# Routed feed-forward stage of a decoder: the gates are laid on 128 rows by transfers, in place of selector products

## The chip, the cores and the metric

The kernel runs on one core of a Trainium2 chip. Its engines are TensorE (PE; its weight loads are shown apart as PEld), VectorE (DVE), ScalarE (ACT), GpSimd (POOL) and the queue engine SyncE (SP), which here only issues transfers (DMA). On-chip memory (SBUF) has 128 rows, called partitions; products land in a second memory (PSUM) of eight banks. The metric is the time of the whole program in device microseconds. A trace is one profiled execution; its span is the time from its first to its last instruction.

## The reference, cut to what matters

The input is x of 16 sequences, 128 tokens, 256 features. Six residual blocks follow, each with a layer norm. The change lies in the third, a feed-forward block with two shared experts of 128 hidden values each and sixteen routed experts of 64:

```python
gs = jnp.einsum('td,ndm->tnm', flat, wg_s)
us = jnp.einsum('td,ndm->tnm', flat, wu_s)
out = jnp.einsum('tnm,nmd->td', jax.nn.silu(gs) * us, wd_s)
logits = (flat @ router_w).astype(jnp.float32)
probs = jax.nn.softmax(logits, axis=-1)
weights, indices = jax.lax.top_k(probs, TOP_K)      # TOP_K = 2 of 16
weights = weights / (weights.sum(axis=-1, keepdims=True) + 1e-09)
comb = jnp.sum(jax.nn.one_hot(indices, N_ROUTED, dtype=x.dtype) * weights[..., None], axis=1)
g = jnp.einsum('td,edm->tem', flat, wg_r)
u = jnp.einsum('td,edm->tem', flat, wu_r)
h = jax.nn.silu(g) * u
h = h * comb[:, :, None]
out = out + jnp.einsum('tem,emd->td', h, wd_r)
```

`comb` is the gate of each token and expert. All sixteen experts are computed for all tokens, and the gate makes most of them zero.

## The kernel before, in words

Each of the six blocks is a stage; the order inside a stage is written out by hand, and semaphores tie the engines together. The routed stage (names `F3` and `f3...`) works in four groups of four sequences, 512 tokens each. Features lie on the partitions, tokens along the row: `f3XT` is x transposed. The hidden values, 256 of the shared and 1024 of the routed experts, are cut into ten chunks of 128 rows: chunks 0 and 1 are shared, chunks 2 to 9 hold two routed experts each, 64 rows per expert. Every product is made of three products of high and low parts (`split3`, lines 85 to 87), so an up step is 12 products of 512 columns and a down step 12 of 256.

The list that `ffn_order` returns is walked by PE, ACT and DVE alike. For chunk c its steps are "u" (PE: up products; ACT: silu into `f3gs`), before the change "s" for c from 2 on (PE: `spread`), "t" (DVE: `product`), "d" of chunk c-2 (PE: down products) and "h" of chunk c-1 (ACT writes the high part `f3hT_h`, DVE the low part `f3hT_l`). So on DVE the low part of chunk c-1 stands behind the product of chunk c, and on PE the down products of c-1 need that low part.

The gates: PE computes the router's logits at a group's start ("l"), ACT and DVE the softmax and the top two ("e", "r"). After chunk 1, PE transposes them (line 1325) to 16 rows of 512 tokens, and DVE copies them from PSUM to `combT` in two parts, high (line 1457) and low (line 1458), on rows 0 to 15 and 32 to 47. `spread` (line 1299) multiplies `combT` by a selector `f3sel` of zeros and ones that puts the gates of experts 2(c-2) and 2(c-2)+1 on 64 rows each. The result lies in a PSUM bank, and `product` makes `f3tt` = silu times up (line 1446) and then `f3h` = `f3tt` times that bank (line 1450). GpSimd and VectorE build the selector in the stage before; `combT` is set to zero once.

SP's program before the stage loads `w_a4` (the next attention's weights) in four pieces; DVE splits them in group 0 after chunks 4 to 7. Piece k may be loaded when piece k-2 is split. Then, once for each of groups 1 to 3, SP copies the next group's x into `f3Xs` (line 1228), which PE transposes after chunk 9 of the group ahead. In the last group, PE also transposes the next stage's x and computes its first keys and queries among the chunks; SP then lays those on partitions (line 1683), 16 partitions per transfer.

Of the kernel before, what the change touches and what calls it, by code (L numbers as in the profile page):

```python
# [89 lines left out]
def program(nc, x_in, ctxT_in, itokT_in, w_a1, w_e1i, w_e1o, w_ffn, w_a4, w_a5, w_e6i, w_e6o,  # L90
# [912 lines left out]
    def mix_vector(v, c, parts, beside=None, between=None):  # L1003
# [138 lines left out]
    F3.gs = m.place("f3gs", [P, 2, GT], F32)  # L1142
    F3.tt = m.place("f3tt", [P, 2, GT], F32)
    F3.h32 = m.place("f3h32", [P, 2, GT], F32)
    F3.combT = m.place("f3combT", [P, GT], F32R)
    F3.lg = m.place("f3lg", [P, GB, R_N], F32)
    F3.pr = m.place("f3pr", [P, GB, R_N + 6], F32)
    F3.mr = m.place("f3mr", [P, GB, R_N + 6], F32)
# [16 lines left out]

    def ffn_order(first, last):

        order = [("l", 0), ("e", 0)]
        if not first:
            order.append(("a", 0))
        order.append(("r", 0))
        for c in range(FC + 1):
            if c < FC:
                x = [("x", k) for k in range(DC)] if last and c == FC - 4 else []
                k = [("nk", k) for k in range(DC)] if last and c == FC - 2 else []
                order += x[:1] + k[:1] + ([("nk evac", 0)] if k else []) + [("u", c)] + x[1:] + k[1:]
                order += ([("s", c)] if c >= SC else []) + ([("nq", 0)] if last and c == FC - 1 else []) + [("t", c)]  # L1180
# [28 lines left out]

        return g * FG + (DC + k + 3)  # L1210

    FL, FT, FX = 0, 1, 2 + FC - SC

    def ffn_last(g):
        return type(g) is int and g == NG - 1

    def ffn_x(g, ch):

        return (FX - 4 if ffn_last(g) else FX) + ch

    def ffn_spread(g, c):
        return c + (DC if ffn_last(g) and c >= FC - 4 else 0)

    def ffn_sync(sp):
        s = F3.s
        with sp.Fori(1, NG) as g:
            sp.wait_ge(s["xt_hi"], g * DC + C1)
            sp.dma_start(F3.Xs[:, :, :], X[:, bass.ds(g * GB, GB), :]).then_inc(s["xs_loaded"], 16)

    def ffn_selector_pool(pool):  # L1230
        s = F3.s

        nc.gpsimd.memset(F3.sel32[:, :, :], 0.0).then_inc(s["sel_pool"], 1)
        pool.wait_ge(s["sel_pool"], 1)
        sel = F3.sel32[:, :, :].rearrange("e c (a m) -> e c a m", a=2)
        for n, row in enumerate((0, LO_ROWS)):
            nc.gpsimd.affine_select(out=sel, in_=sel, compare_op=ALU.not_equal, fill=1.0, base=-row,
                                    pattern=[[-2, FC - SC], [-1, 2], [0, R_MID]], channel_multiplier=1).then_inc(s["sel_pool"], 1)
            if n == 0:
                pool.wait_ge(s["sel_pool"], 2)  # L1240
# [34 lines left out]
    def ffn_tensor(pe, first_keys, first_queries):  # L1275
# [16 lines left out]
        def spread(g, c):

            bank = g_fill(g, ffn_spread(g, c))
            if ffn_last(g) and c >= FC - 2:
                pe.wait_ge(N.s["g_evac"], n_filled(0, NK + c - (FC - 2)))
            if c == SC:
                pe.wait_ge(s["g_evac"], ffn_evac(g, FT))
            nc.tensor.matmul(bank, F3.sel[:, c - SC, :], F3.combT[:, :], start=True, stop=True).then_inc(s["g_full"], 1)

        def down(g, c):
            pe.wait_ge(s["h_ready"], g * FC + c + 1 + C1)
            if c == 0:
# [24 lines left out]
        def steps(g, order):  # L1328
            for kind, c in order:
                if kind == "x":  # L1330
                    transposed_x(g, c)
                elif kind == "l":
                    logits(g)
                elif kind == "u":
                    up(g, c)
                elif kind == "c":
                    gates_transposed(g)
                elif kind == "s":
                    spread(g, c)
                elif kind == "d":  # L1340
                    down(g, c)
                elif kind == "nk":
                    first_keys(c)
                elif kind == "nq":
                    first_queries(c)

        pe.wait_ge(s["sel_ready"], 1)
        ffn_groups(pe, steps)

    def ffn_scalar(act):  # L1350
# [9 lines left out]
        def steps(g, order):  # L1360
            for kind, c in order:
                if kind == "x":
                    transposed_x(g, c)
                elif kind == "e":
                    act.wait_ge(s["g_evac"], ffn_evac(g, FL))
                    nc.scalar.activation(F3.pr[:, :, 0:R_N], F3.lg[:, :, :], ACT.Exp).then_inc(s["soft_exp"], 1)
                elif kind == "u":
                    act.wait_ge(s["gu_full"], g * FC + c + 1)
                    nc.scalar.activation(F3.gs[:, c % 2, :], ps[:, c % 2, :], ACT.Silu).then_inc(s["sg_ready"], 1)
                elif kind == "h":  # L1370
                    if c < SC:
                        act.wait_ge(s["t_done"], g * FC + c + 3)
                    else:
                        act.wait_ge(s["g_evac"], ffn_evac(g, ffn_spread(g, c)))
                    nc.scalar.activation(F3.hT[0][:, c % 3, :], F3.h32[:, c % 2, :], ACT.Identity).then_inc(s["hi_ready"], 1)
                elif kind in ("nk evac", "nq evac"):
                    n_hi_qk(act, 0, kind[1], c)
# [1 line left out]
        for ch in range(DC):  # L1379
            transposed_x(-1, ch)  # L1380
        ffn_groups(act, steps)

    def ffn_selector(v):
        v.wait_ge(F3.s["sel_pool"], 3)
        nc.vector.tensor_copy(F3.sel[:, :, :], F3.sel32[:, :, :]).then_inc(F3.s["sel_ready"], 1)

    def ffn_transposed_x(v, g, ch):
        s = F3.s
# [13 lines left out]
    def ffn_vector_begin(v, ch):  # L1402
        s = F3.s
        if ch == 0:
            nc.vector.memset(F3.combT[:, :].bitcast(F32), 0.0).then_inc(s["sel_ready"], 1)
            nc.vector.memset(F3.pr[:, :, R_N:], -1.0).then_inc(s["sel_ready"], 1)
            v.wait_ge(s["sel_ready"], 3)
        ffn_transposed_x(v, -1, ch)

    def ffn_vector(v, link, of_mixture, following):  # L1410
# [31 lines left out]
        def product(g, c):  # L1442
# [2 lines left out]
            dst = F3.h32 if c < SC else F3.tt  # L1445
            nc.vector.tensor_tensor(dst[:, c % 2, :], F3.gs[:, c % 2, :], ps[:, 2 + c % 2, :], ALU.mult).then_inc(s["t_done"], 1)
            if c >= SC:
                v.wait_ge(s["g_full"], ffn_full(g, ffn_spread(g, c)))
                v.wait_ge(s["t_done"], g * FC + c + 3)
                nc.vector.tensor_tensor(F3.h32[:, c % 2, :], F3.tt[:, c % 2, :], ps[:, 4 + c % 2, :], ALU.mult).then_inc(s["g_evac"], 1)  # L1450
                v.wait_ge(s["g_evac"], ffn_evac(g, ffn_spread(g, c)))

        def gates_transposed(g):
            v.wait_ge(s["g_full"], ffn_full(g, FT))
            src = ps[0:R_N, 4 + FT % 2, :]
            hi, lo = F3.combT[0:R_N, :], F3.combT[LO_ROWS:LO_ROWS + R_N, :]
# [317 lines left out]
    def n_projections(pe):  # L1774
# [370 lines left out]
    with block as block:  # L2145
        @block.sync
        def _(sp):
# [57 lines left out]
        def _(pool):  # L2205
# [62 lines left out]
        def _(v):  # L2268
# [129 lines left out]
```

## Time and profile before

| | |
|---|---|
| median of 3 runs | 1560.12 us (1559.51 to 1562.1) |
| the profiled execution | 1562.81 us, its span 1560.8 us |
| share of the span: PE, PEld, DVE, ACT, POOL | 97%, 84%, 63%, 47%, 13% |
| mean granted clock of TensorE | 0.989 of full speed |
| routed stage | about 679 to 884 us of the span |

Busy PE time is the union of its products, whose ends are modelled: what one product costs in a dense row of products is the distance from its start to the next one's start, not its duration.

### The profile page before, as it was taken

Reading aid. Unit: us, or ns where it says so; the run is one execution under the profiler, and the core shown is the slowest. Engines: PE = TensorE matmul, PEld = TensorE weight load, DVE = VectorE, ACT = ScalarE, POOL = GpSimd, SP = SyncE. Lnnn points to the kernel's source line nnn. Section 1 sums busy time; section 2 is a strip of 40 time slices with the busy share of each in tenths; the row PEclk is TensorE's granted clock in tenths of the full one; section 3 lists DMA queues with packets and bytes.
Section 4 is the critical chain, followed back from the end, with each engine's and each line's share of the span. In section 5 each row is a group of like instructions: output and inputs, shape, how many; then the busy total and the mean of one; then the engine's idle time right before and its main releaser. Section 6 shows DMA issues by size and latency. Waiting matters only on the chain.

```text
span 1560.8 us, 28560 instructions
## 1 busy us (share of the span) xinstructions
PE 1514.9 (97%) x10996; PEld 1316.0 (84%) x11018; DVE 988.6 (63%) x2131; ACT 729.8 (47%) x1874; POOL 203.7 (13%) x215
## 2 busy tenths in 40 slices
PE   7999999899999999999999999999998999999997
PEld 6898988789999999978888867777766988999886
DVE  6777777864554555576666567788886464444547
ACT  4766666622222222223323367788884444444443
POOL 1322322310000000030000034212221300000001
PEclk9999999999999999999999999999999999999999
DMA  6000100011010101100000585677750000000001
GB/s 217 1 15 1 42 2 1 28 40 41 26 36 19 52 27 39 34 1 34 1 13 1 74 139 67 86 101 134 105 79 28 1 28 28 28 27 27 27 0 54
DMA packets 43080, 66.50 MB, mean 43 GB/s; under 512 B 4576, under 2 KB 33504, under 8 KB 42848
## 3 DMA queue, kind: packets, MB, share of 16 engines
q1 hardware_dynamic: 42976, 65.09, 20.0%
q8 instruction: 68, 1.11, 0.3%
q14 instruction: 36, 0.29, 0.1%
HBM read 36.24 MB, written 2.10 MB: 25 GB/s over the span
## 4 chain that ended last, share of the span: by engine, by line
PE 90%; DVE 6%; ACT 2%; issue 1%; DMA 1%; POOL 0%; SPq 0%; DVEq 0%; POOLq 0%; ACTq 0%
PE ps L85 23%; PE ps L86 22%; PE ps L87 22%; PE ps L1859 3%; PE ps L1873 3%; PE ps L1849 2%; PE ps L392 2%; PE ps L404 2%; PE ps L417 2%; PE ps L1904 2%; PE ps L1887 1%; ACT wPr L472 1%; PE ps L1846 1%; PE ps L1895 1%; PE ps L1823 0%
## 5 line engine op out<-in xcount | busy, mean ns | idle before, releaser
L858 ACT ACTIVATE m2hT_h<-ps 128x512 fp32r<-128x512 f32 x128 | 76.7, 599 | 281.4 <-PE ps L87 281.4
L982 DVE TENSOR_TENSOR m6hT_l<-m6h,m6hT_h 128x512 fp32r<-128x512 f32 x128 | 88.5, 691 | 169.5 <-ACT m6hT_h L856 169.5
L984 DVE SCALAR_TENSOR_TENSOR m2hT_l<-ps,m2hT_h 128x512 fp32r<-128x512 f32 x128 | 88.4, 691 | 163.4 <-ACT m2hT_h L858 163.4
L855 ACT ACTIVATE m6h<-ps,m6b 128x512 f32<-128x512 f32 x128 | 88.4, 691 | 202.5 <-PE ps L87 196.2
L1985 ACT ACTIVATE nPr<-ps,negm 128x128 f32<-128x128 f32 x512 | 147.2, 383 | 26.2 <-DVE negm L2088 25.3
L87 PE MATMUL ps<-w_h,m6hT_l 128*128 128x256 f32 x512 | 144.4, 282 | 0.0
L85 PE MATMUL ps<-w_h,m6hT_h 128*128 128x256 f32 x512 | 143.0, 279 | 0.7 <-DVE m6hT_l L982 0.7
L86 PE MATMUL ps<-w_l,m6hT_h 128*128 128x256 f32 x512 | 143.6, 280 | 0.0
L87 PE MATMUL ps<-m2w_h,m2hT_l 128*128 128x256 f32 x448 | 126.8, 283 | 0.0
L86 PE MATMUL ps<-m2w_l,m2hT_h 128*128 128x256 f32 x448 | 126.7, 283 | 0.0
L85 PE MATMUL ps<-m2w_h,m2hT_h 128*128 128x256 f32 x448 | 126.3, 282 | 0.0
L2088 DVE TENSOR_REDUCE negm<-ps 128x4 f32<-128x512 f32 x128 | 88.2, 689 | 48.1 <-PE ps L1849 47.6
L85 PE MATMUL ps<-m6XT_h,w_h 128*128 128x512 f32 x256 | 103.3, 404 | 2.1 <-DVE m6hT_l L982 2.1
L87 PE MATMUL ps<-m6XT_h,w_l 128*128 128x512 f32 x256 | 102.1, 399 | 0.0
L85 PEld LDWEIGHTS ps<-w_h,m6hT_h 128*128 128x128 f32 x512 | 96.7, 189 | 5.9 <-DVE m6hT_l L982 0.9
L86 PE MATMUL ps<-m6XT_l,w_h 128*128 128x512 f32 x256 | 101.3, 396 | 0.0
L86 PEld LDWEIGHTS ps<-w_l,m6hT_h 128*128 128x128 f32 x512 | 96.2, 188 | 5.7
L892 POOL TENSOR_TENSOR rstd<-veps,mhalf 128x4 f32<-128x4 f32 (+1 forms) x9 | 9.7, 1074 | 684.2 <-DVE veps L1041 679.3
L472 ACT ACTIVATE wPr<-ps,negm 128x128 f32<-128x128 f32 x256 | 90.3, 372 | 14.7 <-DVE negm L553 14.7
L87 PEld LDWEIGHTS ps<-w_h,m6hT_l 128*128 128x128 f32 x512 | 96.2, 188 | 0.0
L85 PEld LDWEIGHTS ps<-m2w_h,m2hT_h 128*128 128x128 f32 x448 | 85.5, 191 | 4.8
L317 POOL TENSOR_TENSOR wPr<-wPr,wrec 128x512 f32<-128x512 f32 x64 | 65.9, 1050 | 180.8 <-DVE wrec L558 180.8
(322 smaller groups left out, 4323.6 us busy)
## 6 DMA issues: line engine op xcount, KB each, us to landing
nKm<-nKc_h SPq DMA_DIRECT2D x64, 128.0 KB, 4.5
nQs<-nQc_h SPq DMA_DIRECT2D x64, 128.0 KB, 5.7
raw<-in_w_e1i SPq DMA_DIRECT2D x9, 512.0 KB, 3.2
raw<-in_w_e1o SPq DMA_DIRECT2D x9, 512.0 KB, 3.3
raw<-in_w_e6i SPq DMA_DIRECT2D x9, 512.0 KB, 3.3
raw<-in_w_e6o SPq DMA_DIRECT2D x9, 512.0 KB, 3.3
nKm<-nKc_l SPq DMA_DIRECT2D x32, 128.0 KB, 5.2
nQs<-nQc_l SPq DMA_DIRECT2D x32, 128.0 KB, 6.0
```

The costliest lines, as they stand in the source:

```text
L85: nc.tensor.matmul(out, wh, xh, start=start, stop=False, **kw)
L86: nc.tensor.matmul(out, wh, xl, start=False, stop=False, **kw)
L87: return nc.tensor.matmul(out, wl, xh, start=False, stop=stop, **kw)
L317: nc.gpsimd.tensor_tensor(own, own, scale.unsqueeze(2).broadcast_to([P, QH, S]), ALU.mult).then_inc(s["p_ready"], 1)
L472: last = nc.scalar.activation(W.Pr[:, p % 3, half, j, :], ps[:, WSB[half], j * S:(j + 1) * S], ACT.Exp, bias=negm[:, n % 4, j:j + 1], accu ...
L855: nc.scalar.activation(c.h32[:, u % 2, :], ps[:, u % 2, :], ACT.Gelu, bias=bias)
L858: nc.scalar.activation(c.hT[0][:, ch, :], ps[:, u % 2, :], ACT.Relu).then_inc(c.s["hi_ready"], 1)
L982: last = nc.vector.tensor_tensor(c.hT[1][:, ch, :], c.h32[:, u % 2, :], c.hT[0][:, ch, :].bitcast(F32), ALU.subtract)
L984: last = nc.vector.scalar_tensor_tensor(c.hT[1][:, ch, :], ps[:, u % 2, :], 0.0, c.hT[0][:, ch, :].bitcast(F32), ALU.max, ALU.subtract)
L1859: last = nc.tensor.transpose(ps[:, TB[n % 2], i * S:(i + 1) * S], N.Pr[:, n % 4, i, :], ident[:, :])
L1985: last = nc.scalar.activation(N.Pr[:, i % 4, j, :], ps[:, SB[i % 2], j * S:(j + 1) * S], ACT.Exp, bias=negm[:, i % 4, j:j + 1])
L2088: nc.vector.reduce_max(negm[:, i % 4, :], ps[:, SB[i % 2], :].rearrange("p (h k) -> p h k", h=QH), AX.X, negate=True).then_inc(s["s_max"], 1)
```

## The change

PE no longer multiplies by a selector. DVE copies the transposed gates to rows 0 to 15 of `combT` in one piece. For each routed chunk, SP issues one transfer that reads two rows of `combT` 64 times each and writes 128 rows of 2 KB. There are six targets: four for chunks 2 to 5 and two that chunks 6 to 9 share, so the transfers of chunks 8 and 9 wait until the product of chunk c-2 has read its target. `product` waits for the transfer's semaphore and reads SBUF in place of PSUM. The selector and its building are gone, and with them the waits of the first keys and queries for the spread banks.

```diff
-    F3.combT = m.place("f3combT", [P, GT], F32R)
+    F3.combT = m.place("f3combT", [P, GT], F32)
...
-    F3.sel32 = m2.place("f3sel32", [P, FC - SC, P], F32)
-    F3.sel = r1b.place("f3sel", [P, FC - SC, P], F32R)
+    NGT = 6
...
+    gates4 = Region(nc, n_x0_at, 8 * KB).place("f3gates4", [P, 4, GT], F32)
+    gates2 = r1b.place("f3gates2", [P, 2, GT], F32)
+    F3.gate = [gates4[:, i, :] for i in range(4)] + [gates2[:, i, :] for i in range(2)]
+    F3.laid = [sem(f"f3_laid{i}") for i in range(NGT)]
...
-                order += ([("s", c)] if c >= SC else []) + ([("nq", 0)] if last and c == FC - 1 else []) + [("t", c)]
+                order += ([("nq", 0)] if last and c == FC - 1 else []) + [("t", c)]
...
+    def ffn_gated(g, c):
+
+        return F3.s["gated"], g * (FC - SC) + (c - SC + 1)
+
+    def ffn_place(c):
+
+        i = c - SC
+        return (i, 0, 1) if i < 4 else (4 + i % 2, (i - 4) // 2, 2)
+
+    def ffn_lay_gates(sp, g, chunks):
+        s = F3.s
+        if chunks[0] == SC:
+            sp.wait_ge(s["g_evac"], ffn_evac(g, FT))
+        for c in chunks:
+            i, load, _ = ffn_place(c)
+            if load:
+                sp.wait_ge(*ffn_gated(g, c - 2))
+            rows2 = F3.combT[2 * (c - SC):2 * (c - SC) + 2, :]
+            sp.dma_start(F3.gate[i], rows2.unsqueeze(1).broadcast_to([2, R_MID, GT])).then_inc(F3.laid[i], 16)
 
     def ffn_sync(sp):
         s = F3.s
-        with sp.Fori(1, NG) as g:
+        sp.wait_ge(s["xt_hi"], DC + C1)
+        sp.dma_start(F3.Xs[:, :, :], X[:, GB:2 * GB, :]).then_inc(s["xs_loaded"], 16)
+        with sp.Fori(2, NG) as g:
             sp.wait_ge(s["xt_hi"], g * DC + C1)
             sp.dma_start(F3.Xs[:, :, :], X[:, bass.ds(g * GB, GB), :]).then_inc(s["xs_loaded"], 16)
...
+            ffn_lay_gates(sp, g - 1, range(SC, FC))
+        ffn_lay_gates(sp, NG - 1, range(SC, FC))
...
-            nc.tensor.matmul(bank, F3.sel[:, c - SC, :], F3.combT[:, :], start=True, stop=True).then_inc(s["g_full"], 1)
...
-            nc.vector.memset(F3.combT[:, :].bitcast(F32), 0.0).then_inc(s["sel_ready"], 1)
...
             if c >= SC:
-                v.wait_ge(s["g_full"], ffn_full(g, ffn_spread(g, c)))
+                i, load, loads = ffn_place(c)
+                v.wait_ge(F3.laid[i], g * (16 * loads) + 16 * (load + 1))
                 v.wait_ge(s["t_done"], g * FC + c + 3)
-                nc.vector.tensor_tensor(F3.h32[:, c % 2, :], F3.tt[:, c % 2, :], ps[:, 4 + c % 2, :], ALU.mult).then_inc(s["g_evac"], 1)
-                v.wait_ge(s["g_evac"], ffn_evac(g, ffn_spread(g, c)))
+                nc.vector.tensor_tensor(F3.h32[:, c % 2, :], F3.tt[:, c % 2, :], F3.gate[i], ALU.mult).then_inc(s["gated"], 1)
+                v.wait_ge(*ffn_gated(g, c))
...
-            link(nc.vector.tensor_copy(hi, src))
-            nc.vector.tensor_tensor(lo, src, hi.bitcast(F32), ALU.subtract).then_inc(s["g_evac"], 1)
+            nc.vector.tensor_copy(F3.combT[0:R_N, :], src).then_inc(s["g_evac"], 1)
...
                 load_unit(sp, U_A4, k, w_a4[:, at:at + n], n)
+                if k == 1:
+                    ffn_lay_gates(sp, 0, range(SC, FC - 2))
+            ffn_lay_gates(sp, 0, range(FC - 2, FC))
             sp.wait_ge(stage_done, 2)
             ffn_sync(sp)
```

On SP, from the next attention's weights (`raw<-in_w_a`) to the end of the stage's x copies, the program before reads:

```order
43 L679 DMA raw_50<-in_w_a 128x768
44 L679 DMA raw_51<-in_w_a 128x768
45 L679 DMA raw_50<-in_w_a 128x256
46 L679 DMA raw_51<-in_w_a 128x256
47 L1226 UNCONDITIONAL_BRANCH
48 L1226 ISA
49 L1228 ISA
50 L1228 DMA f3Xs<-X 128x1024
```

and the changed one (`f3gates_160` are the four targets of chunks 2 to 5, `f3gates_161` the two of chunks 6 to 9; what a row waits for is in brackets):

```order
43 L679 DMA raw_50<-in_w_a 128x768 [waits prep_done]
44 L679 DMA raw_51<-in_w_a 128x768 [waits prep_done]
45 L1243 DMA f3gates_160<-f3combT 128x1x512 [waits f3_g_evac]
46 L1243 DMA f3gates_160<-f3combT 128x1x512 x3
47 L1243 DMA f3gates_161<-f3combT 128x1x512 x2
48 L679 DMA raw_50<-in_w_a 128x256 [waits prep_done]
49 L679 DMA raw_51<-in_w_a 128x256 [waits prep_done]
50 L1243 DMA f3gates_161<-f3combT 128x1x512 [waits f3_gated] x2
51 L1248 DMA f3Xs<-X 128x1024 [waits f3_xt_hi,stage_done]
```

Six gate transfers of group 0 now stand ahead of the last two weight pieces, and two more ahead of the first copy of x, which stood right behind the weights before.

On DVE, in group 0 from the copy of the transposed gates to the product of chunk 3, before:

```order
639 L1457 CAST f3combT<-ps 16x512
640 L1458 TENSOR_TENSOR f3combT<-ps,f3combT 16x512
641 L1524 TENSOR_TENSOR f3hT_l<-f3h_148,f3hT_h 128x512
642 L1446 TENSOR_TENSOR f3tt<-f3gs,ps 128x512
643 L1450 TENSOR_TENSOR f3h_148<-f3tt,ps 128x512
644 L1524 TENSOR_TENSOR f3hT_l<-f3h_148,f3hT_h 128x512
```

and changed:

```order
637 L1453 COPY f3combT<-ps 16x512
638 L1519 TENSOR_TENSOR f3hT_l<-f3h_148,f3hT_h 128x512
639 L1442 TENSOR_TENSOR f3tt<-f3gs,ps 128x512
640 L1447 TENSOR_TENSOR f3h_148<-f3tt,f3gates_160 128x512
641 L1519 TENSOR_TENSOR f3hT_l<-f3h_148,f3hT_h 128x512
```

One of the two copies is gone, and the product with the gates (line 1450 before, 1447 now) reads the laid gates; the low part of the chunk before stands behind it as it did.

On PE, at the end of the up products of chunk 2 in group 0, before:

```order
2722 L86 MATMUL ps<-f3XT_l,wF_h 128x512
2723 L87 MATMUL ps<-f3XT_h,wF_l 128x512
2724 L1299 MATMUL ps<-f3combT,f3sel 128x512
2725 L85 MATMUL ps<-wF_h,f3hT_h 128x256
2726 L86 MATMUL ps<-wF_l,f3hT_h 128x256
```

and changed:

```order
2719 L86 MATMUL ps<-f3XT_l,wF_h 128x512
2720 L87 MATMUL ps<-f3XT_h,wF_l 128x512
2721 L85 MATMUL ps<-f3XT_h,wF_h 128x512
2722 L86 MATMUL ps<-f3XT_l,wF_h 128x512
2723 L87 MATMUL ps<-f3XT_h,wF_l 128x512
2724 L85 MATMUL ps<-wF_h,f3hT_h 128x256
2725 L86 MATMUL ps<-wF_l,f3hT_h 128x256
```

The down products of chunk 0 now follow the up products directly; the same holds at the other 31 places.

## Rows read from the trace of the kernel before

**Rows 1.** The page: busy time of PE, and the chain that ended last.

```profile
PE 1514.9 (97%) x10996; PEld 1316.0 (84%) x11018; DVE 988.6 (63%) x2131; ACT 729.8 (47%) x1874; POOL 203.7 (13%) x215
PE 90%; DVE 6%; ACT 2%; issue 1%; DMA 1%; POOL 0%; SPq 0%; DVEq 0%; POOLq 0%; ACTq 0%
```

**Rows 2.** Stretch 690 to 884 us: busy time by engine, granted clock, DMA share, GB/s.

```profile
690.00:884.00 194.00, 190.72 (x1084) 164.40 (x1085) 119.45 (x270) 60.81 (x100) 12.83 (x6) 0.99 0.05 16
```

**Rows 3.** Waits of PE in that stretch: us in total, times, longest.

```profile
PE ps L85 <- DVE f3h L1446: 2.7, 3, 1.9
PE ps L85 <- DVE f3hT_l L1524: 0.8, 3, 0.3
```

**Rows 4.** PE in order of time around two selector products (start, duration), and their group.

```profile
753.38 0.40 PE L1299 MATMUL ps<-f3combT,f3sel 128*128 128x512 f32 x1
753.62 0.29 PE L85 MATMUL ps<-wF_h,f3hT_h 128*128 128x256 f32 x1
...
757.82 0.40 PE L1299 MATMUL ps<-f3combT,f3sel 128*128 128x512 f32 x1
...
L1299 PE MATMUL ps<-f3combT,f3sel 128*128 128x512 f32 x32 | 12.7, 398 | 0.0
```

**Rows 5.** DVE in order of time: copy of the gates, product of chunk 9, groups 0 to 3.

```profile
692.57 0.68 DVE L1457 CAST f3combT<-ps 16x512 fp32r<-16x512 f32 x1
...
727.99 0.69 DVE L1450 TENSOR_TENSOR f3h<-f3tt,ps 128x512 f32<-128x512 f32 x1
...
742.07 0.67 DVE L1457 CAST f3combT<-ps 16x512 fp32r<-16x512 f32 x1
...
777.21 0.69 DVE L1450 TENSOR_TENSOR f3h<-f3tt,ps 128x512 f32<-128x512 f32 x1
...
791.00 0.67 DVE L1457 CAST f3combT<-ps 16x512 fp32r<-16x512 f32 x1
...
826.17 0.69 DVE L1450 TENSOR_TENSOR f3h<-f3tt,ps 128x512 f32<-128x512 f32 x1
...
839.82 0.67 DVE L1457 CAST f3combT<-ps 16x512 fp32r<-16x512 f32 x1
...
878.39 0.69 DVE L1450 TENSOR_TENSOR f3h<-f3tt,ps 128x512 f32<-128x512 f32 x1
```

**Rows 6.** End of group 2 in order of time, DVE and PE.

```profile
826.89 0.69 DVE L1524 TENSOR_TENSOR f3hT_l<-f3h,f3hT_h 128x512 fp32r<-128x512 f32 x1
...
829.59 0.39 PE L85 MATMUL ps<-wF_h,f3hT_h 128*128 128x256 f32 x1 [0.26 <-DVE f3hT_l L1524]
```

**Rows 7.** Transfers, 779 to 782 us: packets, MB, share of 16 engines; time to landing.

```profile
q1 hardware_dynamic: 144, 0.52, 43.1%
f3Xs<-X SPq DMA_DIRECT2D x1, 512.0 KB, 2.9
```

**Rows 8.** Transfers, 1011 to 1016 us: GB/s in 40 slices, then as in rows 7.

```profile
GB/s 131 172 139 131 106 123 98 107 90 164 164 123 115 115 123 90 98 123 180 139 123 115 106 115 98 98 148 156 156 131 98 106 107 90 131 164 148 123 115 115
DMA packets 684, 0.62 MB, mean 124 GB/s; under 512 B 77, under 2 KB 684, under 8 KB 684
q1 hardware_dynamic: 684, 0.62, 117.5%
```

**Rows 9.** Busy time and granted clock (seventh number) around a wait of PE.

```profile
687.90:691.30 3.40, 1.23 (x7) 0.88 (x8) 3.33 (x13) 0.63 (x1) 1.01 (x1) 1.00 0.01 2
691.30:694.70 3.40, 3.40 (x10) 2.63 (x9) 3.17 (x7) 0.00 (x0) 2.17 (x1) 0.53 0.00 0
694.70:698.10 3.40, 3.40 (x21) 3.02 (x20) 2.05 (x3) 1.12 (x2) 3.40 (x1) 0.97 0.00 0
```

**Rows 10.** PE in order of time in the slow stretch.

```profile
692.20 0.63 PE L87 MATMUL ps<-f3XT_h,wF_l 128*128 128x512 f32 x1
692.63 0.63 PE L85 MATMUL ps<-f3XT_h,wF_h 128*128 128x512 f32 x1
```

**Rows 11.** The selector's copy on DVE: duration in ns, start in us.

```profile
L1385 DVE CAST f3sel<-f3sel x1: 684/684/684, 404.7 to 404.7; 128x1024 fp32r<-128x1024 f32 x1
```

More of the change, by code:

```diff
@@ L1154, in program @@
     F3.r = m.place("f3r", [P, GB, D], F32)
-    m2 = Region(nc, M2.end, r2.end - M2.end)
-    F3.sel32 = m2.place("f3sel32", [P, FC - SC, P], F32)
-    F3.sel = r1b.place("f3sel", [P, FC - SC, P], F32R)
+    NGT = 6
+    n_x0_at = r2.start + 45120
+    assert m.at <= n_x0_at
+    gates4 = Region(nc, n_x0_at, 8 * KB).place("f3gates4", [P, 4, GT], F32)
+    gates2 = r1b.place("f3gates2", [P, 2, GT], F32)
+    F3.gate = [gates4[:, i, :] for i in range(4)] + [gates2[:, i, :] for i in range(2)]
+    F3.laid = [sem(f"f3_laid{i}") for i in range(NGT)]
     F3.s = signals("f3", "xs_loaded xt_hi g_full g_evac soft_exp comb_ready gu_full sg_ready t_done hi_ready h_ready "
-                         "d_full r_done ln_var rstd_ready x_done sel_pool sel_ready")
+                         "d_full r_done ln_var rstd_ready x_done gated pad_ready")
     assert m.at <= n_at
-    FG = 2 + FC - SC + DC
-    LO_ROWS = 32
-    F_LINKS = 19 + 2 * GB
+    FG = 2 + DC
+    F_LINKS = 18 + 2 * GB
     def ffn_order(first, last):
@@ L1210, in ffn_evac @@
         return g * FG + (DC + k + 3)
-    FL, FT, FX = 0, 1, 2 + FC - SC
+    FL, FT, FX = 0, 1, 2
     def ffn_last(g):
@@ L1217, in ffn_x @@
     def ffn_x(g, ch):
-        return (FX - 4 if ffn_last(g) else FX) + ch
-    def ffn_spread(g, c):
-        return c + (DC if ffn_last(g) and c >= FC - 4 else 0)
+        return FX + ch
+    def ffn_gated(g, c):
[13 more added lines that the diff above has]
+            sp.dma_start(F3.gate[i], rows2.unsqueeze(1).broadcast_to([2, R_MID, GT])).then_inc(F3.laid[i], 16)
     def ffn_sync(sp):
         s = F3.s
-        with sp.Fori(1, NG) as g:
+        sp.wait_ge(s["xt_hi"], DC + C1)
+        sp.dma_start(F3.Xs[:, :, :], X[:, GB:2 * GB, :]).then_inc(s["xs_loaded"], 16)
+        with sp.Fori(2, NG) as g:
             sp.wait_ge(s["xt_hi"], g * DC + C1)
             sp.dma_start(F3.Xs[:, :, :], X[:, bass.ds(g * GB, GB), :]).then_inc(s["xs_loaded"], 16)
[L1230 to L1240, printed above, removed]
+            ffn_lay_gates(sp, g - 1, range(SC, FC))
+        ffn_lay_gates(sp, NG - 1, range(SC, FC))
     def ffn_pool(pool):
@@ L1290, in up @@
             last.then_inc(s["gu_full"], 1)
[L1292 to L1298, printed above, removed]
-            nc.tensor.matmul(bank, F3.sel[:, c - SC, :], F3.combT[:, :], start=True, stop=True).then_inc(s["g_full"], 1)
         def down(g, c):
@@ L1337, in steps @@
                     gates_transposed(g)
-                elif kind == "s":
-                    spread(g, c)
                 elif kind == "d":
@@ L1345, in steps @@
                     first_queries(c)
-        pe.wait_ge(s["sel_ready"], 1)
         ffn_groups(pe, steps)
@@ L1373, in steps @@
                     else:
-                        act.wait_ge(s["g_evac"], ffn_evac(g, ffn_spread(g, c)))
+                        act.wait_ge(*ffn_gated(g, c))
                     nc.scalar.activation(F3.hT[0][:, c % 3, :], F3.h32[:, c % 2, :], ACT.Identity).then_inc(s["hi_ready"], 1)
@@ L1381, in ffn_scalar @@
         ffn_groups(act, steps)
-    def ffn_selector(v):
-        v.wait_ge(F3.s["sel_pool"], 3)
-        nc.vector.tensor_copy(F3.sel[:, :, :], F3.sel32[:, :, :]).then_inc(F3.s["sel_ready"], 1)
     def ffn_transposed_x(v, g, ch):
@@ L1404, in ffn_vector_begin @@
         if ch == 0:
-            nc.vector.memset(F3.combT[:, :].bitcast(F32), 0.0).then_inc(s["sel_ready"], 1)
-            nc.vector.memset(F3.pr[:, :, R_N:], -1.0).then_inc(s["sel_ready"], 1)
-            v.wait_ge(s["sel_ready"], 3)
+            nc.vector.memset(F3.pr[:, :, R_N:], -1.0).then_inc(s["pad_ready"], 1)
+            v.wait_ge(s["pad_ready"], 1)
         ffn_transposed_x(v, -1, ch)
@@ L1455, in gates_transposed @@
             src = ps[0:R_N, 4 + FT % 2, :]
-            hi, lo = F3.combT[0:R_N, :], F3.combT[LO_ROWS:LO_ROWS + R_N, :]
-            link(nc.vector.tensor_copy(hi, src))
-            nc.vector.tensor_tensor(lo, src, hi.bitcast(F32), ALU.subtract).then_inc(s["g_evac"], 1)
+            nc.vector.tensor_copy(F3.combT[0:R_N, :], src).then_inc(s["g_evac"], 1)
         def sums_of(g):
@@ L1801, in first_keys @@
                 pe.wait_ge(prep_done, U_A5)
-            pe.wait_ge(F3.s["g_evac"], ffn_evac(NG - 1, ffn_spread(NG - 1, FC - 4 + ch)))
             project(0, "k", A4.wk, ch, *of_x(0))
         def first_queries(ch):
-            pe.wait_ge(F3.s["g_evac"], ffn_evac(NG - 1, ffn_spread(NG - 1, FC - 2 + ch)))
             project(0, "q", A4.wq, ch, *of_x(0))
@@ L2225, in _ @@
             pool.wait_ge(stage_done, 1)
-            ffn_selector_pool(pool)
             mix_pool(pool, M2)
@@ L2319, in _ @@
             v.sem_inc(stage_done, 1)
-            of_mixture = mix_vector(v, M2, m2, lambda: (ffn_selector(v), ffn_vector_start(v)), lambda ch: ffn_vector_begin(v, ch))
+            of_mixture = mix_vector(v, M2, m2, lambda: ffn_vector_start(v), lambda ch: ffn_vector_begin(v, ch))
             def start_n():
```

## Prediction

> **What bounds the kernel now.** I read the page first: PE is busy for 97% of the span and makes up 90% of the chain that ended last [rows 1]. Then the stretch of the routed stage: from 690 to 884 us PE is busy for 190.7 of 194 us, DVE for 119, ACT for 61, and the transfer engines for 5% [rows 2]. The waits of PE there come to 2.7 us for the first products of each group and 0.8 us for the last low parts of `f3hT` [rows 3]. So PE bounds the stage, DVE has room, and the transfers hardly exist. An instruction taken off PE is time gained, unless something takes PE's place.
>
> **What is removed.** From a selector product to the product behind it PE takes 753.62 - 753.38 = 0.24 us (its duration of 0.40 overlaps with its neighbours), and there are 32 of them [rows 4]: 32 x 0.235 = 7.5 us. One chunk now takes 757.82 - 753.38 = 4.44 us and would take 4.20. DVE's second copy of the gates (as long as the first, 0.67 us, four times), the clearing of `combT` and the selector's copy [rows 11] go too, and GpSimd's building of it. I cost these at nothing: PE does not wait for the copies (its next step needs the product of chunk 0, ahead of them), and the selector's copy, 0.68 us at 404 us, lies in a stage where PE bounds too. Should they be on the path, they are at most 4 x 0.67 + 0.7 for the selector and no more than 0.7 for the clearing (as long a row as other steps of 0.69), 4.1 us more of gain.
>
> **What is added.** Per group eight transfers of 128 x 2 KB = 256 KB each, issued by SP when DVE has copied the gates. Call the time from one landing to the next T, and the fixed part of a transfer F. F comes from the copy of x into `f3Xs`: 512 KB in 2.9 us from issue to landing, with 0.431 x 16 x 3 us = 20.7 us of engine time, so 25.3 GB/s for each engine and 1.3 us for its share [rows 7]. F = 2.9 - 1.3 = 1.6 us, and 0.1 for SP's wait: 1.7. The gates of chunk 9 land 1.7 + 8T after the copy of the gates ends.
>
> What waits: DVE's product with the gates of chunk c. Behind it on DVE stand the low part of chunk c-1 and the product of c+1; PE's down products of c-1 need that low part. On SP the transfers of chunks 8 and 9 wait for the products of chunks 6 and 7, and what stands behind them waits too. In the middle of a group there is slack, at the end there is none: PE begins the last down step 829.59 - 826.17 = 3.4 us after the product of chunk 9 and even waits 0.26 us for it [rows 5, 6]. So a group is longer by what the last product is later.
>
> From the end of the gates' (first) copy to the product of chunk 9 there are now 727.99 - 693.25 = 34.7, 777.21 - 742.74 = 34.5, 826.17 - 791.67 = 34.5 and 878.39 - 840.49 = 37.9 us [rows 5], in sum 141.6 us (the last group holds work of the next stage). Without selector products they would be shorter by 7.5 in all. With transfers that are slower than PE the sum is 4 x (1.7 + 8T). The break-even lies near T = 4.2 us, or 63 GB/s for one transfer.
>
> **How large is T?** No row shows a transfer that reads two rows 64 times. Lower bound: all 16 engines at their 25.3 GB/s, 256 KB / 405 GB/s = 0.65 us. Upper bound: transfers that write 16 neighbouring partitions. They run at a mean of 124 GB/s with the engines more than fully taken (117.5%) [rows 8], 7.8 GB/s for each partition; two partitions at that rate give 16.9 us. Which is nearest? [...] The two rows that a gate transfer reads are neighbours (2(c-2) and the next), thus most likely behind one door, however many engines fetch: T = 256 KB / 25.3 GB/s, about 10.3 us. I take that. [...]
>
> [...]
>
> **The sum.** 4 x (1.7 + 82.4) - 141.6 = 194.8 us. Group 0 adds two things. The two weight pieces now stand between the gates of chunks 7 and 8 and share the transfer engines: 2 x 128 KB at 16 engines, 0.7 us. And the first `f3Xs` copy, which had stood ahead, follows the gates of chunk 9; PE's transposes wait for it, and with them ACT's and DVE's copies that stand ahead of the last high and low part: 1.6 us. That is 197.1. **PE's clock**: PE stands for most of each group, some 6 us between a chunk's 4.2 us of work. The trace shows what follows: after a stretch in which PE was busy for 1.23 of 3.40 us the granted clock is 0.53, so mostly the 1.2 GHz level, and full again after it [rows 9]; products of 512 columns then come every 0.43 us, not 0.23 [rows 10]. Inside a group half clock is hidden, since 4.2 x 0.43 / 0.23 = 7.9 us of work still fit into 10.3. At each end the two last down steps (12 x 0.12 = 1.4 us each) and the start of what follows run at it: about 1.8 us, four times, 7 us. In all +204 us. The profiled execution took 1562.8 (span 1560.8 and 2.0 around it), 2.7 above the median of 1560.1; the change applies to either, so 1560.1 + 204 = **1764 us**, +13%.
>
> **Rivals.** (1) *Two engines, two doors.* The source's outermost count is 2 (rows), the target's 128. If the work is split by the outermost count, two engines fetch one row each at 25.3 GB/s: 128 KB each, T = 5.2 us. If the two rows do not share a door, the sum is 4 x (1.7 + 41.6) - 141.6 + 2.3 = +33.9 us, 1594 us, and PE's idle time of 1 us a chunk leaves the clock up. For it: rows 8 speak of writes alone. [...]
>
> (2) *Transfers hidden: faster.* If all 16 engines take part and neighbours do not share, T = 0.65 us plus SP's issue. The gates of chunk 2 land 1.7 + 0.65 = 2.4 us after the copy; the product with them is due 34.5 - 7 x 4.44 = 3.4 us after it [rows 4, 5], and PE gains its 7.5 us: 1552.6 us. It decides for T below 4.2. For it: the transfer engines are idle for 95% of the stage [rows 2], and one such engine is fast. Against: it needs 63 GB/s out of two neighbouring rows, 2.5 times what one engine shows.
>
> (3) *Concentration as bad as in rows 8 per partition.* T = 16.9: 4 x (1.7 + 135) - 141.6 + 2.3 = +408 us, with the clock about 1975 us.
>
> (4) *No measurable change*: a T of 4.1 to 4.3 us. Nothing in the rows points there.
>
> **Chances.** My forecast (T of 9.5 to 11) 0.66; two doors 0.20; between 5.6 and 9.5 us 0.04; worse than 11 us 0.05; hidden 0.04; no change 0.01. What a measurement of this kernel tells from no change is about 0.2%. So slower 0.95, same 0.01, faster 0.04. The forecast's own range goes from T = 9.6 with little loss by the clock (4 x 78.5 - 141.6 + 2.3 = +175, 1735) to T = 10.8 and twice that loss (about 1795). Since it holds but two thirds, the range takes in the case of two doors, 1588 to 1604: 1588 to 1795, a wide gap with little in the middle.
>
> **What will show it.** PE: no line of selector products; the busy share of the stage at some 45% and long waits of its down products for the low part `f3hT_l` (right), or none (rival 2). DVE: idle ahead of the product that reads `f3gates`, released by the transfer, some 6 us for each chunk (1 us in rival 1), growing from the first chunk on. The chain that ended last: some 330 us of transfers `f3gates<-f3combT` in it. Transfers: few engines busy (2 of 16, a share of 0.12, if the work is split by the outermost count) and about 25 GB/s through the stage, 50 in rival 1. Landings: the sixth of a burst some 6 x 10.3 us after issue. The clock at 0.5 for parts of the stage. Stages before 690 us should stay as they are. I am wrong if reads of neighbours are not limited as writes are, or if a fetch of the same row 64 times is served in some faster way.

## The result, and the profile after

The changed kernel takes a median of 1763.28 us (1762.01 to 1767.86, 4 runs), beside 1561.11 us (1559.51 to 1564.08, 4 runs) for the kernel before: a ratio of 1.1298, 95% interval 1.127 to 1.1326. The forecast was 1764. The profiled execution took 1762.22 us with a span of 1760.4, 199.6 more than the span before.

The page of the changed kernel: busy time, PE and the granted clock in 40 slices, the chain that ended last, and two groups with the idle time ahead of them behind the second bar.

```profile
PE 1560.9 (89%) x10986; PEld 1352.6 (77%) x10986; DVE 983.9 (56%) x2125; ACT 731.3 (42%) x1874; POOL 200.4 (11%) x212
...
PE   7999998999999997656576667899999899999997
...
PEclk9999999999999999777787878999999999999999
...
PE 72%; DMA 14%; SPq 6%; DVE 5%; ACT 2%; issue 1%; POOL 0%; DVEq 0%; POOLq 0%; ACTq 0%
PE ps L85 18%; PE ps L86 18%; PE ps L87 18%; DMA f3gates<-f3combT 11%; SPq L1243 5%; PE ps L1852 3%; PE ps L1866 2%; DMA raw<-in_w_a 2%; PE ps L392 2%; PE ps L1842 2%; PE ps L1897 2%; PE ps L417 2%; PE ps L404 2%; DMA f3Xs<-X 1%; PE ps L1880 1%
...
L85 PE MATMUL ps<-wF_h,f3hT_h 128*128 128x256 f32 x160 | 64.7, 404 | 145.6 <-DVE f3hT_l L1519 145.6
...
L1447 DVE TENSOR_TENSOR f3h<-f3tt,f3gates 128x512 f32<-128x512 f32 x32 | 22.1, 692 | 236.6 <-DMA f3gates<-f3combT 236.5
```

PE was the chain by 90% [rows 1] and is 72% now. The gates' transfers (11%) and SP's issue of them (line 1243, 5%), 282 us together, stand in it. PE waits 145.6 us for the low parts `f3hT_l`, and DVE, one step earlier, 236.5 us for the gates. Beside [rows 3] and [rows 5], where PE waited 0.8 us for those low parts and DVE's product came from PSUM, that is the new wait.

The waits of the stretch 690 to 1090 us: engine, line, waited for, us in total, times, longest.

```profile
DVE f3h L1447 <- DMA f3gates<-f3combT: 236.5, 31, 10.7
...
PE ps L85 <- DVE f3hT_l L1519: 145.6, 30, 11.9
```

DVE in order of time, as in [rows 5], with the first products of group 1.

```profile
690.91 0.68 DVE L1453 COPY f3combT<-ps 16x512 f32<-16x512 f32 x1
...
777.73 0.69 DVE L1447 TENSOR_TENSOR f3h<-f3tt,f3gates 128x512 f32<-128x512 f32 x1 [7.67 <-DMA f3gates<-f3combT]
...
793.22 0.67 DVE L1453 COPY f3combT<-ps 16x512 f32<-16x512 f32 x1
...
806.23 0.69 DVE L1447 TENSOR_TENSOR f3h<-f3tt,f3gates 128x512 f32<-128x512 f32 x1 [8.96 <-DMA f3gates<-f3combT]
...
817.09 0.69 DVE L1447 TENSOR_TENSOR f3h<-f3tt,f3gates 128x512 f32<-128x512 f32 x1 [8.65 <-DMA f3gates<-f3combT]
...
879.01 0.69 DVE L1447 TENSOR_TENSOR f3h<-f3tt,f3gates 128x512 f32<-128x512 f32 x1 [7.79 <-DMA f3gates<-f3combT]
...
894.23 0.67 DVE L1453 COPY f3combT<-ps 16x512 f32<-16x512 f32 x1
...
979.14 0.69 DVE L1447 TENSOR_TENSOR f3h<-f3tt,f3gates 128x512 f32<-128x512 f32 x1 [7.35 <-DMA f3gates<-f3combT]
...
993.82 0.67 DVE L1453 COPY f3combT<-ps 16x512 f32<-16x512 f32 x1
...
1079.88 0.69 DVE L1447 TENSOR_TENSOR f3h<-f3tt,f3gates 128x512 f32<-128x512 f32 x1 [7.79 <-DMA f3gates<-f3combT]
```

In group 1 the first product comes 806.23 - 793.89 = 12.3 us after the copy's end, the eighth 72.8 us later: a transfer lands every 72.8 / 7 = 10.4 us. 31 of the 32 products wait for their own transfer, so DVE and PE merely follow. (The one that doesn't is that of chunk 7 in group 0, where DVE splits weights meanwhile.)

The transfers from 800 to 840 us, as in [rows 7].

```profile
DMA packets 502, 1.03 MB, mean 26 GB/s; under 512 B 8, under 2 KB 8, under 8 KB 500
...
q1 hardware_dynamic: 500, 1.01, 11.9%
```

26 GB/s with 11.9% of the engine time used: two of sixteen engines, hardly ever idle, would show 12.5%.

The stage in windows, columns as in [rows 2] (the seventh number is the granted clock), with three pieces of 3.4 us around one wait.

```profile
806.90:810.30 3.40, 2.59 (x12) 2.60 (x13) 1.40 (x3) 0.63 (x1) 0.00 (x0) 0.50 0.14 30
810.30:813.70 3.40, 3.40 (x11) 2.68 (x11) 0.00 (x0) 0.00 (x0) 0.00 (x0) 0.54 0.12 25
813.70:817.10 3.40, 1.06 (x5) 0.54 (x3) 0.01 (x1) 0.60 (x1) 0.00 (x0) 0.97 0.13 28
690.00:1088.00 398.00, 243.60 (x1061) 205.44 (x1059) 114.64 (x265) 62.86 (x99) 11.82 (x5) 0.78 0.13 30
```

After a wait, 145.6 / 30 = 4.9 us on average, PE begins a chunk's work mostly at half clock (0.50, then 0.54) and is granted the full clock (0.97) only when that work is nearly over. Over the whole stage the clock is 0.78, against 0.99 [rows 2].

### The profile page after: what moved, and what is told of

It is laid out like the page before. It is cut to its first block, busy times and chain, and to the rows that moved or that the text cites. A ratio compares the mean times of both kernels' runs of the same rounds, so it can differ in the third digit from the quotient of the medians.

```text
span 1760.4 us, 28524 instructions
## 1 busy us (share of the span) xinstructions
PE 1560.9 (89%) x10986; PEld 1352.6 (77%) x10986; DVE 983.9 (56%) x2125; ACT 731.3 (42%) x1874; POOL 200.4 (11%) x212
## 4 chain that ended last, share of the span: by engine, by line
PE 72%; DMA 14%; SPq 6%; DVE 5%; ACT 2%; issue 1%; POOL 0%; DVEq 0%; POOLq 0%; ACTq 0%
PE ps L85 18%; PE ps L86 18%; PE ps L87 18%; DMA f3gates<-f3combT 11%; SPq L1243 5%; PE ps L1852 3%; PE ps L1866 2%; DMA raw<-in_w_a 2%; PE ps L392 2%; PE ps L1842 2%; PE ps L1897 2%; PE ps L417 2%; PE ps L404 2%; DMA f3Xs<-X 1%; PE ps L1880 1%
## 5 line engine op out<-in xcount | busy, mean ns | idle before, releaser
L85 PE MATMUL ps<-wF_h,f3hT_h 128*128 128x256 f32 x160 | 64.7, 404 | 145.6 <-DVE f3hT_l L1519 145.6
L85 PEld LDWEIGHTS ps<-wF_h,f3hT_h 128*128 128x128 f32 x160 | 44.9, 280 | 158.7 <-DVE f3hT_l L1519 158.5
L1447 DVE TENSOR_TENSOR f3h<-f3tt,f3gates 128x512 f32<-128x512 f32 x32 | 22.1, 692 | 236.6 <-DMA f3gates<-f3combT 236.5
L1370 ACT ACTIVATE f3gs<-ps 128x512 f32<-128x512 f32 x40 | 23.9, 597 | 189.2 <-PE ps L87 189.2
```

Source lines behind the costliest of these rows:

```text
L85: nc.tensor.matmul(out, wh, xh, start=start, stop=False, **kw)
```

## The experiments

Each edit below is a difference to the changed kernel. Two questions are open after the result: is it the rows' place or the count of engines that holds a transfer at 25 GB/s, and did PE's 7.5 us come off at all? A time without a range is that of a single run; the time beside a result is that of the kernel before on the same chip.

**`e1_rows8`: the two rows of a chunk 8 apart.** DVE's last router product writes the gates in another order, so that the transposed rows of a chunk's two experts are i and i+8. One transfer still carries both.

```diff
...
-            rows2 = F3.combT[2 * (c - SC):2 * (c - SC) + 2, :]
+            rows2 = F3.combT[c - SC:c - SC + 9:8, :]
...
+            apart = F3.comb[:, :, :].rearrange("p b (j i) -> p b i j", j=2)
+            own = F3.own[:, :, :].rearrange("p b (i j) -> p b i j", j=2)
...
```

> The gates are transposed in another order, so that the two experts of a chunk stand on rows 8 apart (i and i+8) and not side by side; the transfers are otherwise the changed kernel's. [...] Theory 'row' (a row that is fetched again and again gives only 12.8 GB/s, or each of the two engines is slow by itself): T stays at 10.4 us and the total at 1763 us.

Measured: 1600.55 us (1600.27 to 1601.77, 4 runs) beside 1560.55, a ratio of 1.0264 (1.0234 to 1.0294). That is 6.6 us above the 1594 that rival 1 works out with T = 5.2 us, and far below the 1763 of theory 'row'. Its transfers from 700 to 720 us, and DVE in group 2:

```profile
DMA packets 575, 1.09 MB, mean 55 GB/s; under 512 B 11, under 2 KB 86, under 8 KB 574
...
q1 hardware_dynamic: 574, 1.08, 14.3%
```

```profile
811.04 0.67 DVE L1457 COPY f3combT<-ps 16x512 f32<-16x512 f32 x1
...
829.19 0.69 DVE L1451 TENSOR_TENSOR f3h<-f3tt,f3gates 128x512 f32<-128x512 f32 x1 [1.11 <-DMA f3gates<-f3combT]
834.46 0.69 DVE L1451 TENSOR_TENSOR f3h<-f3tt,f3gates 128x512 f32<-128x512 f32 x1 [1.68 <-DMA f3gates<-f3combT]
...
855.09 0.69 DVE L1451 TENSOR_TENSOR f3h<-f3tt,f3gates 128x512 f32<-128x512 f32 x1 [2.94 <-DMA f3gates<-f3combT]
```

Twice the rate (the slices of that view read 49 to 53 GB/s but for a few with other transfers), still with about the share of two engines; a landing every 5.2 us ((855.09 - 818.65) / 7, from the first product of the group to the eighth). Four fifths of the loss are gone by the place of a row alone.

**`e2_rows33` and `e2b_rows65`: how far apart.** DVE copies the rows twice, to rows 0 to 15 and to 32 to 47 (or 64 to 79), and the transfer takes its second row from the second copy.

```diff
-            rows2 = F3.combT[2 * (c - SC):2 * (c - SC) + 2, :]
+            r = 2 * (c - SC)
+            rows2 = F3.combT[r:r + 34:33, :]
...
+            link(nc.vector.tensor_copy(F3.combT[0:R_N, :], src))
+            nc.vector.tensor_copy(F3.combT[32:32 + R_N, :], src).then_inc(s["g_evac"], 1)
```

> VectorE writes the gates' rows twice, to rows 0 to 15 and to rows 32 to 47 (0.7 us more per group), and each transfer takes its first row from the first and its second from the second copy, 33 rows apart. [...]

> As the run with rows 33 apart, but the second copy of the gates stands on rows 64 to 79 and the two rows of a transfer are 65 apart. [...]

Measured: 1749.72 us with 33 apart beside 1560.55, 1599.31 with 65 apart beside 1560.09 (the author's estimates were 1765, the changed kernel and 0.7 us more in each group for the second copy, and 1603, `e1_rows8` and the same). Transfers from 700 to 720 us, first of `e2_rows33`, then of `e2b_rows65`:

```profile
DMA packets 270, 0.56 MB, mean 28 GB/s; under 512 B 4, under 2 KB 4, under 8 KB 269
```

```profile
DMA packets 502, 1.02 MB, mean 51 GB/s; under 512 B 8, under 2 KB 12, under 8 KB 501
```

DVE in group 1 of `e2_rows33`:

```profile
804.27 0.69 DVE L1448 TENSOR_TENSOR f3h<-f3tt,f3gates 128x512 f32<-128x512 f32 x1 [8.79 <-DMA f3gates<-f3combT]
...
873.27 0.69 DVE L1448 TENSOR_TENSOR f3h<-f3tt,f3gates 128x512 f32<-128x512 f32 x1 [8.43 <-DMA f3gates<-f3combT]
```

So it isn't distance: 33 apart is nearly as slow as 1 apart (a landing every 69.0 / 7 = 9.9 us, beside 10.4), while 65 and 8 apart give double. These two kernels differ in nothing but the rows of the second copy. What counts is which two rows a transfer reads: rows 1 and 33 apart come at 25.2 and 26.6 GB/s by the landings, rows 8 and 65 apart at some 50 (256 KB in 5.2 us).

**`e3_one_row`: sixteen engines at the same rows.** Each chunk's gates come by two transfers, each of one row 64 times, out of the same neighbouring rows.

```diff
+            for j in range(2):
+                row = F3.combT[2 * (c - SC) + j:2 * (c - SC) + j + 1, :]
+                sp.dma_start(F3.gate[i][j * R_MID:(j + 1) * R_MID, :],
+                             row.unsqueeze(1).broadcast_to([1, R_MID, GT])).then_inc(F3.laid[i], 16)
```

> Two transfers per chunk, each reads one row of combT 64 times and writes 64 rows; the outermost count is now 64 on both sides, so that all 16 engines can take part. [...] Theory 'two engines' (only the number of engines limits): a chunk's gates take under 2 us, they are hidden, the total is 1550 to 1556 us. Theory 'row' (12.8 GB/s for one row): the rows go one after the other, 20 us per chunk, the total near 2085 us.

Measured: 1701.21 us beside 1560.55. That is far above the 1550 to 1556 of theory 'two engines', far below the 2085 of theory 'row', and below the author's estimate of 1755 to 1770 for gates that still take 10.3 us a chunk. Transfers from 700 to 720 us:

```profile
DMA packets 364, 0.62 MB, mean 31 GB/s; under 512 B 70, under 2 KB 70, under 8 KB 363
...
q1 hardware_dynamic: 363, 0.60, 89.5%
```

All sixteen engines are busy for 89.5% of their time, 7.5 times the share of the changed kernel, for 31 GB/s in place of 26. The rate of group 1, 782 to 852 us in 40 slices, in which SP has no other transfers:

```profile
GB/s 0 34 29 26 28 28 28 27 25 28 25 62 39 26 27 28 26 29 27 37 37 67 28 26 28 27 26 28 26 52 54 27 27 27 26 29 35 29 26 15
```

Most slices read 25 to 29 GB/s: sixteen engines (a share of 89.5%) get hardly more out of a pair of neighbours than two do (11.9%, a mean of 26 GB/s). The slices of 52 to 67 stand right ahead of the products of chunks 3, 5 and 7 (803.38, 820.51 and 835.92 us). What was read faster in them, and where the 62 us come from that this version is below the changed kernel, no run shows.

**`e7_one_row8`: both edits at once** (one row for each transfer, the rows 8 apart).

> One row per transfer on 16 engines, from SBUF, with the two experts of a chunk on rows 8 apart. [...]

Measured: 1593.21 us beside 1560.46, 7 less than `e1_rows8` and also 7 below the author's estimate of 1600 to 1690, for a T between the 5.2 us of `e1_rows8` and 10.3. Transfers from 700 to 720 us:

```profile
DMA packets 695, 1.16 MB, mean 58 GB/s; under 512 B 137, under 2 KB 137, under 8 KB 694
...
q1 hardware_dynamic: 694, 1.14, 90.8%
```

Again a busy share of 90% for little: 58 GB/s, where two engines had some 50.

**`e5_hbm_pair` and `e4_hbm_one_row`: no SBUF rows to read.** SP first writes the 16 rows (32 KB) to main memory and then reads the gates from there; in `e5_hbm_pair` with the two-row transfer of the change, in `e4_hbm_one_row` with the two transfers of `e3_one_row`.

```diff
...
+            sp.dma_start(F3.rowsT, F3.combT[0:R_N, :]).then_inc(F3.spilled, 16)
+            sp.wait_ge(F3.spilled, g * 16 + 16)
...
-            rows2 = F3.combT[2 * (c - SC):2 * (c - SC) + 2, :]
+            rows2 = F3.rowsT[2 * (c - SC):2 * (c - SC) + 2, :]
```

> The same detour by main memory, but the laying transfers are the changed kernel's: one per chunk, two rows 64 times each, outermost count 2. If two engines do it and the door is gone, each has 128 KB at about 25 GB/s: T is 5.2 us as with rows 8 apart, 4 x 2.2 us more for the detour, the total 1600 to 1612 us. If all 16 engines did it, under 1558 us. If only the repeated row counts, 1763 us or more.

> The gates' 16 rows are first written to main memory (32 KB) and each row is then read from there 64 times, in transfers of one row each on 16 engines; numbers and sizes of the laying transfers are those of the run with one row per transfer. If the limit is the SBUF door, it is gone: a chunk's gates land in under 2 us, but the first come one round trip later, some 4.5 us after the copy where 4.8 are free; the total is 1552 to 1558 us. If fetching one row again and again is slow wherever it lies, T stays between 8 and 11 us and the total between 1690 and 1780 us.

Measured: 1612.73 us (0.7 above the range expected) and 1555.95 us (inside it), beside 1560.09. Transfers of `e5_hbm_pair`, 700 to 720 us:

```profile
DMA packets 491, 1.00 MB, mean 50 GB/s; under 512 B 8, under 2 KB 8, under 8 KB 490
...
q1 hardware_dynamic: 490, 0.99, 13.1%
```

With no rows of SBUF to read the two-row transfer still gets 50 GB/s with the share of two engines. That is a second limit, behind the first. `e4_hbm_one_row` has neither. Its transfers from 741 to 751 us (KB each, us to landing), and DVE there:

```profile
DMA packets 757, 1.26 MB, mean 126 GB/s; under 512 B 157, under 2 KB 157, under 8 KB 754
...
f3gates<-f3rowsT SPq DMA_DIRECT2D x11, 128.0 KB, 3.0
...
f3rowsT<-f3combT SPq DMA_DIRECT2D x1, 32.0 KB, 1.6
```

```profile
741.34 0.67 DVE L1459 COPY f3combT<-ps 16x512 f32<-16x512 f32 x1
...
747.00 0.69 DVE L1453 TENSOR_TENSOR f3h<-f3tt,f3gates 128x512 f32<-128x512 f32 x1 [1.57 <-DMA f3gates<-f3rowsT]
```

In this group the first gates are there 747.00 - 742.01 = 5.0 us after the copy, detour included. DVE waits once in each group (2.0, 1.6, 1.7 and 3.0 us), for the first gates, then no more.

**`e6_no_transfers`: the ceiling.** No gates are fetched; DVE multiplies `f3tt` by itself, so the gates are left out of the result. DVE's work is the same.

```diff
     def ffn_lay_gates(sp, g, chunks):
+        return
...
-                nc.vector.tensor_tensor(F3.h32[:, c % 2, :], F3.tt[:, c % 2, :], F3.gate[i], ALU.mult).then_inc(s["gated"], 1)
+                nc.vector.tensor_tensor(F3.h32[:, c % 2, :], F3.tt[:, c % 2, :], F3.tt[:, c % 2, :], ALU.mult).then_inc(s["gated"], 1)
```

> No gate transfer is issued and none is waited for; VectorE multiplies silu times up by itself in place of the gates, at the same length, so the gates' part of the computation is left out. All the rest is the changed kernel. Every theory: the 32 selector products at 0.235 us are off PE, 7.5 us, 1552 to 1555 us. If the copies taken from VectorE lay on the path too, 2 to 4 us less, near 1550 us. If the selector products were hidden, 1560 us.

Measured: 1553.28 us (1548.69 to 1555.4, 8 runs) beside 1560.55, a ratio of 0.9952 (0.9932 to 0.9973), which is 4 to 11 us.

**`e8_hbm_again`: `e4_hbm_one_row` timed again, over twelve runs.**

> The kernel that lays one row per transfer from main memory, timed against the kernel before in five rounds. The one look gave 1556 us. Every theory that holds by now: the selector products' 7.5 us gained, less the waits for the first gates of each group (6 us of waits on DVE, of which PE sees about 3), so 1554 to 1558 us, a ratio of 0.996 to 0.999.

Measured: 1557.78 us (1554.23 to 1559.79, 12 runs) beside 1560.46, a ratio of 0.9982 (0.9972 to 0.9992). The stretch 690 to 884 us of `e8_hbm_again`, then of `e6_no_transfers`, columns as in [rows 2]:

```profile
690.00:884.00 194.00, 186.98 (x1076) 160.75 (x1076) 118.77 (x274) 60.50 (x100) 12.63 (x6) 0.99 0.22 62
```

```profile
690.00:884.00 194.00, 187.36 (x1076) 162.23 (x1076) 119.50 (x278) 60.58 (x100) 12.83 (x6) 0.98 0.09 20
```

With the detour this is the one complete version faster than both kernels, by 0.18% at the middle of the interval, which lies at the edge of what a measurement tells here. Its median is 4.5 us above that of `e6_no_transfers`. The profiled spans are equal (1553.2 us each), but they hide this: the profiled run is the second fastest of its twelve, that of `e6_no_transfers` the second slowest of its eight. Within these two traces the stage, from the first copy's end to the last product, takes 874.80 - 693.06 = 181.7 us and 873.06 - 693.73 = 179.3 us. PE's waits for the low parts, of `e8_hbm_again` and then of `e6_no_transfers`:

```profile
PE ps L85 <- DVE f3hT_l L1525: 4.7, 8, 1.0
```

```profile
PE ps L85 <- DVE f3hT_l L1518: 2.1, 4, 0.5
```

So 2.4 us of the 4.5 stand in the stage, where PE waits 2.6 us more for low parts, which stand behind the late first gates of each group. The rest stays open.

## Why the prediction was right

**PE's gain was real and small.** Forecast 7.5 us for the selector products; `e6_no_transfers` measures 1560.55 - 1553.28 = 7.3, with an interval of 4 to 11. DVE's freed copy, the clearing and the selector's copy, costed at nothing with 4.1 us as a bound, brought nothing to be seen; the interval leaves room for some 3 us.

**T.** The step everything hung on was to give two neighbouring rows together the 25.3 GB/s that an engine had in [rows 7], 10.3 us for 256 KB. No run shows this term as it was made: rows 7 and 8 are writes into SBUF, and that reads of neighbours share one engine's rate was the author's estimate. In its place the trace shows a landing every 10.4 us, 25.2 GB/s for the two rows. The runs show that it goes by the rows: at the same bytes, transfers and engines, moving one source row from 1 to 8 or 65 away halves T to 5.2 us (`e1_rows8`, `e2b_rows65`), and 33 away leaves 9.9 us or 26.6 GB/s (`e2_rows33`; the 26 and 28 of the views hold some other traffic). No run shows the 9.6 us at the lower end of the forecast's own range either; the nearest are these 9.9 us. The fixed part was right as well: 1.7 + 10.3 = 12.0 us to the first product, 12.3 measured.

**Which rival was true in part.** Rival 1 said that two engines carry the transfer, and it was right on that, wrong on the rows: neighbours had 25.2 GB/s together, where rows 8 apart had 50. The share of 11.9% in the changed kernel is that of 1.9 engines, the 13.1% of `e5_hbm_pair` (50 GB/s, no rows of SBUF) that of 2.1, while transfers of one row show 90%, from the same rows (`e3_one_row`) as from rows 8 apart (`e7_one_row8`). So two engines' time goes into a transfer whose outermost count is 2, as that rival supposed. Its price was +33.9 us; with the rows 8 apart `e1_rows8` measures 1600.55 - 1560.55 = +40. The rival's clock that stays up is 0.94 there from 690 to 930 us, against 0.78 in the changed kernel's stage. Group 2 there takes 855.09 - 811.71 = 43.4 us from the copy's end to the last product, where the rival had 1.7 + 41.6 = 43.3. Rival 2 (hidden, PE keeps its gain) needed many engines and no rate that the rows share: `e4_hbm_one_row` is that case, 126 GB/s at a share of 37.3% from 741 to 751 us. Rival 3 (7.8 GB/s for each row) is out: the two rows had 25.2 together.

**The sum, term by term**, on the two profiled executions. From the end of the copy to the product of chunk 9: 777.73 - 691.59, 879.01 - 793.89, 979.14 - 894.90 and 1079.88 - 994.49, in sum 340.9 us against 141.6 [rows 5], +199.3. Forecast: 4 x (1.7 + 82.4) = 336.4 and 0.7 for the weight pieces, thus +195.5. T was 0.1 to 0.15 us too low, 32 times over, about 4. Between a group's last product and the next copy's end there were 14.75, 14.46 and 14.32 us [rows 5], and there are 16.16, 15.89 and 15.35: +3.9, where the clock and the late `f3Xs` copy had been put at 7 + 1.6. This term was sized double. PE did wait 8.0 us for the late `f3Xs` copy, but that end lost 16.16 - 14.75 = 1.4 us, no more than the next one without a late copy, so its 1.6 us don't show. The clock's loss is 1.3 us at each of three ends, not 1.8 at four. (Of the forecast's 1.2 GHz a row shows 512 columns in 0.43 us [rows 10], 1.19 a nanosecond; the granted clock stands in the profile as a share of full speed, 0.53 in [rows 9].) The rest: the first copy ends 1.7 us earlier than before, which is not the change's doing (693.1 and 693.7 in `e8_hbm_again` and `e6_no_transfers`), and what follows the last product is 1.9 us shorter (2.3 us in `e6_no_transfers`, so a small loss at the fourth end may be hidden in it). 199.3 + 3.9 - 1.7 - 1.9 = 199.6. The errors of the two terms, 4 us too little in T and 5 too much at the ends, cancelled by luck; the forecast of +204, beside +199.6 in the profiled executions and +202.2 in the medians, was nearer than its terms deserved. The upper end of the forecast's own range is misadded, without effect: 4 x (1.7 + 86.4) - 141.6 + 2.3 + 14 = +227 makes 1787, not 1795.

**The signs.** PE's long waits for `f3hT_l`, DVE's of 6 us and more for each chunk, a share of 0.12 at 25 GB/s and a clock near 0.5 came as named. DVE's waits did not grow through a group: in group 1 the first two, 9.0 and 8.7 us, are the longest. Nor did two sizes come: some 282 us of transfers and SP's issue in the chain, not 330; and PE's busy share of the stage is 243.6 / 398 = 61%, not 45%, since instructions at half clock are longer. The forecast knew those rows [rows 10] and left them out of the share.

**What stays open.** Why rows 33 apart are read in 9.9 us and neighbours in 10.4, worth 14 us of the whole. And in `e3_one_row` the landings come 5.5 to 10 us apart with slices of 52 to 67 GB/s ahead of some; the cause is not shown. Most variants ran once; their differences of 12 us and more are clear, since the runs of one kernel lie within some 5 us of their median; the 7 us between `e7_one_row8` and `e1_rows8` are less so.

## What to carry to other kernels

Cost a broadcast by transfers from where it is read, not from its bytes or the idle engines: a few source rows can share a rate, here about 25 GB/s for two rows 1 or 33 apart and 50 for rows 8 or 65 apart, and 256 KB a chunk against 4.2 us of matmul needs 63. If such a broadcast is wanted, take the rows from main memory (a 32 KB detour, 5.0 us to the first gates) by transfers of one row each, not of two: 1555.95 us against 1612.73 here. And look first at what is to be gained: all 32 selector products cost PE 7.5 us, and the version that fetches nothing at all won 7.3.

## What the runs showed of the hardware that was not expected

- More engines at the same rows bring little: out of neighbouring rows 16 engines had 31 GB/s in the mean and 25 to 29 in most slices, two engines 26; with the rows 8 apart 58 against about 50. They show a busy share of 90% meanwhile, so a high share of the transfer engines is no sign of bytes moved.
- Main memory showed no such narrow place at this size: one row of 2 KB, read 64 times by each transfer, came at a mean of 126 GB/s over 10 us of `e4_hbm_one_row`, with slices up to 336.
- PE stood 145.6 us for low parts, yet its busy time rose from 1514.9 to 1560.9 us with 32 products fewer: standing makes the work behind it longer too. A product of line 85 with `f3hT_h` took 0.29 us [rows 4] and takes 404 ns in the mean now; the stage's clock is 0.78.
